# TensorE's order in a two-layer graph kernel: graph 0's first piece ahead of graph 1's attended sums, the sixth heads behind them, key turning and transposes last

## The reference

```python
h = jnp.maximum(_layernorm(x), 0.0)
x = x + adj @ (h @ weight) + bias                    # layer 0
h = jnp.maximum(_layernorm(x), 0.0)                  # layer 1
feat_proj = (h @ fc_w + fc_b)                        # 8 heads of 256
q = feat_proj @ q_w + q_b;  k = feat_proj @ k_w + k_b
logits = q + swap(k);  masked = logits + (1 - adj) * -1e9
attn = softmax(leaky_relu(masked, 0.01))
out = (attn @ feat_proj) @ fp_w + fp_b + h
x = x + sigmoid(out)
```

## Time and profile before

| | before |
|---|---|
| median of 3 executions | 1424.37 us (1424.36 to 1426.49) |
| profiled execution, its own time | 1423.27 us |
| its span, first to last instruction | 1421.5 us |
| PE busy | 1400.3 us (99%), 9624 instructions |
| DVE busy | 1262.0 us (89%) |
| ACT busy | 1111.6 us (78%) |
| POOL busy | 1105.7 us (78%) |
| mean granted TensorE clock | 0.998 of full speed |

### The profile page before, as it was taken

One profiled execution on the slowest core, in us unless ns is written; L12 is line 12 of the kernel. 1 busy time (PEld: TensorE's weight loads), 2 busy tenths in 40 slices (PEclk: granted clock), 3 DMA queues, 4 the chain that ended last, 5 costly groups with the idle time before them and its releaser, 6 DMA issues.

```text
span 1421.5 us, 32663 instructions
## 1 busy us (share of the span) xinstructions
PE 1400.3 (99%) x9624; PEld 1289.0 (91%) x9624; DVE 1262.0 (89%) x4536; ACT 1111.6 (78%) x3428; POOL 1105.7 (78%) x1291
## 2 busy tenths in 40 slices
PE   8989999999999999999999999999999999999997
PEld 7889999999999999999999999999999999999976
DVE  7988989989989989998999999999999999899875
ACT  4868787787788787787887877887887887877764
POOL 4778778778878778778778778788788788788754
PEclk9999999999999999999999999999999999999999
DMA  6213223223133133133133133232232232232111
GB/s 224 106 61 106 72 85 104 65 90 104 57 98 104 52 103 104 52 104 103 53 104 95 61 104 88 67 104 82 73 104 77 78 104 74 82 104 72 48 49 49
DMA packets 43245, 123.13 MB, mean 87 GB/s; under 512 B 5968, under 2 KB 9680, under 8 KB 43216
## 3 DMA queue, kind: packets, MB, share of 16 engines
q1 hardware_dynamic: 42928, 122.77, 27.6%
q10 hardware_dynamic: 288, 0.01, 0.0%
HBM read 105.46 MB, written 17.30 MB: 86 GB/s over the span
## 4 chain that ended last, share of the span: by engine, by line
PE 92%; DVE 3%; DMA 1%; issue 1%; ACT 1%; POOL 1%; SPq 0%; POOLq 0%; DVEq 0%; ACTq 0%
PE gbank L404 45%; PE ybank L404 24%; PE bank L404 10%; PE tbank L521 7%; PE bank L449 4%; PE bank L479 2%; DVE att L881 1%; DMA late<-fc_wT_dram 1%; PE gbank L424 1%; PE bank L457 1%; DVE att L888 0%; DVE g_lo L864 0%; ACT att L1300 0%; DVE pT_lo L871 0%; POOL att L1624 0%
## 5 line engine op out<-in xcount | busy, mean ns | idle before, releaser
L1300 ACT ACTIVATE att<-att 128x128 f32<-128x128 f32 x1024 | 397.8, 392 | 48.4 <-DVE att L888 48.3
L1617 POOL TENSOR_TENSOR att<-late,t_pos 128x512 f32<-128x512 f32 x256 | 331.4, 1296 | 131.6 <-PE tbank L521 127.7
L404 PE MATMUL gbank<-m_hi,hT_lo 128*128 128x512 f32 (+1 forms) x1024 | 404.9, 395 | 0.4 <-DVE g_lo L864 0.4
L404 PE MATMUL gbank<-m_hi,hT_hi 128*128 128x512 f32 (+1 forms) x1024 | 373.4, 365 | 0.0
L404 PE MATMUL gbank<-m_lo,hT_hi 128*128 128x512 f32 (+1 forms) x1024 | 372.4, 364 | 0.0
L1624 POOL TENSOR_TENSOR att<-att,rinv 128x512 f32<-128x512 f32 x256 | 295.2, 1153 | 94.4 <-DVE rinv L893 94.3
L864 DVE TENSOR_TENSOR g_lo<-gbank,g_hi 128x512 fp32r<-128x512 f32 x448 | 302.2, 677 | 51.1 <-ACT g_hi L1293 46.5
L881 DVE TENSOR_SCALAR_CACHE_REDUCE att<-att,kq_sb 128x128 f32<-128x128 f32 x1024 | 291.1, 338 | 33.4 <-POOL att L1617 33.4
L1293 ACT ACTIVATE g_hi<-gbank 128x512 fp32r<-128x512 f32 x448 | 259.7, 594 | 50.2 <-PE gbank L404 50.2
L1307 ACT ACTIVATE pT_hi<-tbank 128x512 fp32r<-128x512 f32 x256 | 152.9, 597 | 142.2 <-PE tbank L521 139.1
L404 PE MATMUL ybank<-g_hi,pT_lo 128*128 128x256 f32 x889 | 249.7, 281 | 3.1 <-DVE g_lo L864 2.4
(11 more groups left out here) (123 smaller groups left out, 2860.5 us busy)
## 6 DMA issues: line engine op xcount, KB each, us to landing
late<-key_rows SPq DMA_DIRECT2D x128, 512.0 KB, 6.1
g_in<-graph_dram SPq DMA_DIRECT2D x64, 512.0 KB, 3.4
out_dram<-ends SPq DMA_DIRECT2D x63, 256.0 KB, 4.5
att<-fc_wT_dram SPq DMA_DIRECT2D x4, 256.0 KB, 5.8
late<-fp_w_dram SPq DMA_DIRECT2D x4, 256.0 KB, 5.5
ends<-fp_w_dram SPq DMA_DIRECT2D x2, 512.0 KB, 7.7
late<-fc_wT_dram SPq DMA_DIRECT2D x2, 512.0 KB, 9.4
key_rows<-rows SPq DMA_DIRECT2D x64, 8.0 KB, 1.4
```

Source lines behind the costliest of these rows:

```text
L404: mm = pe.matmul(out_ap, w, m, start=first and n == 0, stop=last and n == len(terms) - 1)
L1300: e = act.activation(a[:, s], a[:, s], ACT.Exp, scale=-1.0, bias=a[:, CH + h:CH + h + 1], accum_out=esum[j][c][:, h:h + 1])
L1617: gp.tensor_tensor(a, keys[q][:, j, c * HC:(c + 1) * HC, :], t_pos[q][:, j, :].unsqueeze(1).broadcast_to([P, HC, P]), ALU.add)\
```

## The change

Four things are altered, all of them orders; no instruction is added or taken away.

1. In the ring, and in all lists of PE, B1 and B2 change places: B1 is now projected first and uses bank 2 behind A2, B2 uses bank 3 behind the last head of graph 1.
2. In PE's loop step, A0 stands ahead of both attended sums of graph 1, `sixth_heads` directly behind them, and only then come `turn_keys` and `transpose_p(i, 0, 0)`.
3. In DVE's loop step, `key_rows_out` moves back behind `add_feats`, and the low part of the sixth heads is taken before that of B1.
4. In `finish`, PE's, DVE's and ACT's lists are adapted in the same way; both last heads of pair 63 come directly one after the other.

```diff
-RING = (..., (THERE, 1), (A0, 0), (SIXTH, 0), (B2, 0), (B1, 0))
+RING = (..., (THERE, 1), (A0, 0), (SIXTH, 0), (B1, 0), (B2, 0))
 # PE, step(i, q)
                 last_head(i + 1, (q + 1) % U, 1)
+                project(i, q, A0)
                 attend(i - 1, (q + 2) % U, 1, 0)
+                attend(i - 1, (q + 2) % U, 1, 1)
+                sixth_heads(i, q)
                 turn_keys(i + 1, (q + 1) % U)
-                project(i, q, A0)
-                attend(i - 1, (q + 2) % U, 1, 1)
                 transpose_p(i, 0, 0)
-                sixth_heads(i, q)
-                project(i, q, B2)
+                project(i, q, B1)
                 transform(i + 2, (q + 2) % U)
                 transpose_p(i, 0, 1)
-                project(i, q, B1)
+                project(i, q, B2)
                 attend(i, q, 0, 0)
 # PE, begin, pairs 0 to 3: B1 and B2 change places, as in
-                project(1, 1, B2)
                 project(1, 1, B1)
+                project(1, 1, B2)
 # PE, finish, pair 61
                 last_head(62, 2, 1)
+                project(61, 1, A0)
                 attend(60, 0, 1, 0)
                 transpose_p(61, 0, 0)
                 attend(60, 0, 1, 1)
-                project(61, 1, A0)
                 turn_keys(62, 2)
+                sixth_heads(61, 1)
                 transform(63, 0)
-                sixth_heads(61, 1)
+                project(61, 1, B1)
+                transpose_p(61, 0, 1)
                 project(61, 1, B2)
-                transpose_p(61, 0, 1)
-                project(61, 1, B1)
 # PE, finish, pairs 62 and 63
                 project(62, 2, A1)
-                attend(61, 1, 1, 0)
                 transpose_p(61, 1, 1)
+                project(62, 2, A2)
                 h_ready(63)
                 last_head(63, 0, 0)
-                project(62, 2, A2)
+                last_head(63, 0, 1)
+                project(62, 2, A0)
+                attend(61, 1, 1, 0)
                 attend(61, 1, 1, 1)
-                last_head(63, 0, 1)
+                turn_keys(63, 0)
                 transpose_p(62, 0, 0)
-                turn_keys(63, 0)
-                project(62, 2, A0)
                 sixth_heads(62, 2)
-                project(62, 2, B2)
                 project(62, 2, B1)
                 transpose_p(62, 0, 1)
+                project(62, 2, B2)
...
 # ACT, finish (its loop step and its begin stay as they are)
                 exp(61, 0, 1)
+                last_high(62, 2, 1)
                 pT_high(61, 0, 0)
+                g_high(61, A0)
                 exp(61, 1, 0)
-                last_high(62, 2, 1)
-                g_high(61, A0)
```

More of the change, by code:

```diff
@@ L734, in finish @@
                 sixth_heads(63, 0)
+                project(63, 0, B1)
+                transpose_p(63, 0, 1)
                 project(63, 0, B2)
-                transpose_p(63, 0, 1)
-                project(63, 0, B1)
                 attend(63, 0, 0, 0)
@@ L1131, in step @@
                 add_feats(i - 1, (q + 2) % U)
+                key_rows_out(i + 1)
                 leaky(i, 1, 0)
@@ L1141, in step @@
                 pT_low(i, 0, 1)
-                g_low(i, B1)
+                g_low(i, SIXTH)
             def finish():
                 mask_min(61, 1, 0, 1)
-                g_low(60, SIXTH)
+                g_low(60, B1)
                 inverse(60, 1, 1)
@@ L1190, in finish @@
                 pT_low(61, 1, 1)
+                leaky(62, 0, 1)
+                inverse(62, 0, 0)
                 keys_queries(63, 0, 0)
                 last_low(63, 0, 0)
-                leaky(62, 0, 1)
-                inverse(62, 0, 0)
+                keys_queries(63, 0, 1)
                 g_low(62, A1)
+                g_low(62, A2)
                 mask_min(62, 2, 1, 1)
                 add_feats(61, 1)
+                key_rows_out(63)
+                last_low(63, 0, 1)
                 leaky(62, 1, 0)
-                g_low(62, A2)
-                keys_queries(63, 0, 1)
-                last_low(63, 0, 1)
                 g_low(62, A0)
-                key_rows_out(63)
                 leaky(62, 1, 1)
```

25 lines of the change are left out of this document (12 added, 13 removed).

## The result

The changed kernel takes 1434.23 us (median of 5 runs, 1431.79 to 1434.96) against 1424.73 of the kernel before (5 runs, 1424.36 to 1426.49): a ratio of 1.006 with the interval 1.0046 to 1.0074. It is slower, by 0.6%, and outside the predicted range of 1416.4 to 1427.0. The profiled execution took 1434.23 us with a span of 1432.3, 10.9 us longer than before's 1421.5.

The account below looks back on a forecast made before the run. The prediction took PE's instructions, not waits, to bound the loop (57 of the 64 pairs). Its terms, 0 + 0 + 1.0 - 3.0 - 1.0 = -3.0 us, took 1424.4 to 1421.4 us, range 1416.4 to 1427.0.

Parts of the forecast that it names:

- The price of PE's new order: Loop step on PE: turning and transposes side by side save no surcharge; 0, bounds -5 us and +1 us.
- The second case: Loop step on PE: the surcharge is saved too, -3.0 - 5, giving 1416.5 us; chance 0.10.
- Play in the loop step: Loop: later turning, copies and key loads still arrive before PE would wait, with about one us of play; 0.
- the fifth rival: Loop: keys come too late and PE waits at the last heads; 1427 to 1438 us, chance 0.17.
- The beginning: Pair 1: ACT takes B2 late, delaying exp and DVE's inverse; PE's pair 3 wait grows +1.0 us, bounds 0 and +1.35.
- The end: Last pairs: pair 63's keys come earlier, -3.0 us with pair 61 included; the clock staying up gives another -1.0.
- The part for pair 61: Finish: transform of pair 63, now behind the sixth heads, no longer fills PE's wait for A1's low part; +0.5 us.
- The clock: Last pair: shorter PE waits keep the granted clock at its upper level; -1.0 us, bounds 0 and -1.6.
- The third case: End: the clock falls all the same behind PE's waits; -2.0 us, 1422.4 us, chance 0.15.
- The first case: Whole kernel: the terms hold as summed, -3.0 us with range -4.5 to -1.5, giving 1421.4 us; chance 0.50.

Follow-up runs that it names:

- n1: Kernel before with only PE's loop step and DVE's copy of the key rows in the new order; 1432.97 us against 1421.62, ratio 1.0077.
- k1: Changed kernel with the loop's key turning directly behind A0 and DVE's key-row copy back behind A1's low part; 1429.89 us, ratio 1.0039 to the kernel before.
- e2: Changed kernel with POOL's finish list normalising pairs 58 and 60 ahead of masks of pairs 59 and 61; 1430.05 us, ratio 1.0043 to the kernel before.
- e1: Changed kernel with ACT's lists of the first two pairs taking B1 ahead of B2, as PE does; 1431.36 us, ratio 1.0053 to the kernel before.
- l2: Changed kernel with the old loop step of PE and DVE's key copy, and ACT's first two pairs in new order; 1421.48 us, ratio 0.9985.
- l3: As l2, with PE's transform of pair 63 also back ahead of the sixth heads of pair 61; 1419.87 us, ratio 0.9964 to the kernel before.
- e3: Changed kernel with PE's transform of pair 63 back ahead of the sixth heads of pair 61; 1428.92 us, ratio 1.0044 to the kernel before.
- l1: Changed kernel with PE's loop step and DVE's copy of the key rows put back as before; 1423.96 us, ratio 1.0 to the kernel before.
- s1: Kernel before with only B1 and B2 exchanged, in the ring and PE's lists; 1424.61 us against 1421.62, ratio 1.0021.
- e4: Changed kernel with the three repairs of e1, e2 and e3 together; 1424.55 us, ratio 1.0004 to the kernel before.

## Why the prediction was wrong

**The price of PE's new order (0): right.** The four transposes and the turning together take 0.46 us and the product behind them 0.32; the usual step went from 21.51 to 21.49. The surcharge is not saved, since the turning holds the array for 0.11 with a transpose behind it. The second case (0.10) is out. Not foreseen was that the quick steps of the last section are absent from the new order; that is worth 1.1 us below.

**Play in the loop step (0): this is the step that failed.** The times in it were close: write 0.7 instead of 0.6 us behind the turning, loads 2.6 instead of 2.0, mask at 8.7 instead of about 8.2. The landing near 720.0 was already later than the start of POOL's mask before, 718.43, so the wait of POOL followed from the prediction's own numbers. It said "I follow this through POOL's mask and DVE's minimum to the last heads of the next step and find about one us of play. No cost in the loop, then: 0." The working behind that one microsecond is not given. Inside the loop the play held in all but three of the 49 steps from pair 8 to 57. What was not followed is the other instruction that POOL has behind the masks, `normalise`, and the list that has masks ahead of it where the loop has not: `finish`, for pairs 58 and 60. In place of the 0 the runs show 4.1 us in one step, 1.0 at the transposes of pair 60 and, in this execution, 1.3 in the loop. n1 (loop order alone: 4.0 us from pair 59 to 60), k1 (keys early, list as it is: 0.3) and e2 (list mended, keys late: 0.4) show both halves of the cause; at this place either one alone costs almost nothing.

So the fifth rival had the right mechanism, late keys, and the wrong place and price. It asked what each 0.1 us per step costs in 57 steps; what came was 4 us once and 1 us once more, where the loop meets the finish. The other 2.5 us of the loop are 1.3 in three longer steps (21.61, 22.05 and 22.10) and, for 1.1 more, quick steps (last section) that the kernel before had and this one has not: of 49 steps, ten of 21.45 and eight of 21.33 are 2.0 us less than at 21.51, and the changed kernel's 21.49 gives 1.0 of that back.

**The beginning (+1.0): right in mechanism, mis-sized, 3.6.** ACT's wait, DVE's wait ahead of the inverse (0.8) and the wait of PE are as described. The step "PE's wait there grows by the same" is off: DVE's two `leaky` came to lie beside two long instructions of POOL, had to take turns with them and took 2.40 instead of 1.30, and the clock fell behind the longer wait. Its upper bound of 1.35 left out both. e1 shows that all of it hangs on the order of two calls in ACT's list. That they take turns with POOL was not tested by itself; but the second `leaky` took 1.79 us in all six kernels that have the exchange without ACT's repair, and 0.68 to 0.70 in the other six.

**The end (-3.0 and -1.0 for the clock).** The chain of pair 63's keys came forward as planned: the copy ran at 1391.49, which less the 13.65 of its pair is 3.6 ahead of the earlier trace rows; l2 and l3, where the loop leaves it alone, win 3.3 and 3.1 us from pair 60 to the end. The size forecast for the chain is near; the forecast for the whole end is not. k1, with early keys, the transform still moved and the clock falling as in the kernel before, wins 1.5 instead of 3.0; l2, the same with the clock not falling, 3.3 instead of 4.0. The part for pair 61 was mis-sized: +0.5 in the sum; the wait grew by 1.7, and putting the transform back is worth 1.3 (e3), with a ratio of 0.9964 for l3 against 0.9985 for l2. In the changed kernel this gain is spent by pairs 60 to 63, which lose 3.1 (1.3 by the transform, 1.0 by the late keys, the rest not traced), so that the finish as a whole costs 0.3.

**The clock.** I expected the upper level to stay near the end. In the changed kernel it fell there, 0.83 and then 0.50 from 1404 to 1406; in l2 it stayed at 1.00 with nearly the same waits. Of the nine profiles with the new finish five have the fall there and four have not, and no single edit parts the two groups. Within one kernel, l2, the mean clock runs from 1.000 to 0.995. The third case, given 0.15, was thus underrated and looks like a matter of the run and not of the kernel; with one profile of each kernel that is not shown.

**The chances.** The first case was given 0.50 and "about three in five" of it beyond 0.2%, which is 0.30 and not the 0.33 of the sum; it alters nothing.

The sum of the terms as they were measured, 3.6 + 2.5 + 4.1 + 3.1 - 2.8 and 0.4 from the start, is the 10.9 of the span.

## What to carry to other kernels

When a step is moved later within a loop, follow what arrives late to every instruction that is queued behind its waiter, on that engine and in every list that takes over from the loop: a prologue or an epilogue that was tuned around the old arrival may put something needed at once behind it. An order of pieces that is written out by hand for several engines has to be exchanged in all of them, the first pairs' lists too. A change with parts that win and parts that lose is worth taking apart: here the exchange and the finish, kept without the new loop step and with two repairs, beat the kernel before by 0.36% and the changed one by about 1%. And where a single wait can bring a fall of the clock or not, compare two profiles place by place with the granted clock beside them, before a difference is put down to an edit.

## What the runs showed of the hardware

**A wait does not decide the clock by its length.** At the beginning PE waited 2.36 us in the changed kernel and the clock fell to 0.59 and 0.56; it waited 2.30 us at the same instruction in e3 and 2.36 in l1 and s1, and in those three the windows behind it grant 1.00. In all twelve kernels PE waits 2.04 us ahead of the key turning near 87 us; only in l3 does the clock fall behind it (0.50 from 88 to 90). Near the end, in k1 and in l2, PE had the same two waits ahead of the same windows, each with four transposes between them. First k1, then l2; windows of 2 us, clock behind POOL's figure:

```profile
1398.00:1400.00 2.00, 1.12 (x7) 1.15 (x8) 2.00 (x5) 1.59 (x7) 2.00 (x2) 0.87 0.00 0
1400.00:1402.00 2.00, 2.00 (x10) 1.81 (x9) 1.54 (x10) 0.00 (x0) 2.00 (x3) 0.50 0.04 8
```

```profile
1388.00:1390.00 2.00, 1.05 (x9) 1.08 (x10) 2.00 (x5) 1.66 (x8) 2.00 (x2) 1.00 0.00 0
1390.00:1392.00 2.00, 2.00 (x14) 1.69 (x13) 1.61 (x10) 0.00 (x0) 2.00 (x3) 1.00 0.03 8
```

The waits were 0.61 and 1.28 us in k1, where the clock fell, and 0.85 and 1.28 in l2, where it did not. A forecast can hold a fall as a chance, not as a term. The Trainium skill (TensorE: Matmul & The Clock Gate, Part 1) says that idling throttles the clock; every fall here does stand behind idle time of PE, but the same idle time is also seen without a fall.

**Quick steps.** In some steps 256-column products start 0.113 us apart instead of 0.118, in groups of 11, 33 or more, and the step takes 21.45 or 21.33 us instead of 21.51, at a granted clock of 1.00 in both. Of the 49 steps from pair 8 to 57 the kernel before has 18 of them, l1 34, l2 18, l3 17, s1 44, k1 19, and the six kernels in which the turning stands directly ahead of the transposes (the changed one, e1, e2, e3, e4, n1) none in 294. What sets them is open. k1 and the changed kernel differ only in the place of the turning and of DVE's copy, so that place decides whether they come. In s1 they are worth 5.5 us against 49 steps of 21.51, which is more than most effects that were looked for here.

**The spread within a kernel.** Executions of one kernel lie 4.5 to 6.4 us apart in l1, l2 and s1. In l2 most of that goes with the granted clock: the mean clock of its eleven executions runs from 1.000 (1418.57 and 1418.88 us) to 0.995 (1424.97 us), and 0.005 of 1420 us is 7.1, by estimate. In l1 the same holds less closely. In s1 executions with 0.997 lie anywhere from 1421.42 to 1424.63, so something else takes part, perhaps the quick steps; that was not shown.
